# Turning h with transposing DMAs and moving the sum q_rot ahead of the maxima, in a cross-attention kernel on Trainium2

## The chip, the cores and the metric

The kernel runs on one core of a Trainium2 chip. The time is the device time of one execution in microseconds; the number quoted is the median of three runs. TensorE (PE), VectorE (DVE), ScalarE (ACT), GpSimd (POOL) and SyncE (SP) each run their own instruction stream and are tied together by semaphores alone. In this kernel SyncE does nothing but issue DMAs.

## The reference

Cross-attention with a residual, for 32 batches of 512 rows of x and 77 rows of context, width 512, 16 heads of 32:

```python
h = x * rsqrt(mean(x * x, -1) + EPS) * norm_w
q = rope(h @ Wq.T);  k, v = encoder_out @ Wkv.T;  k = rope(k)
attn = softmax(q . k / sqrt(32));  out = attn . v
return x + out @ Wo.T
```

x, the context, the weights and the result are float32. `rope(t)` is `t * cos + rotated(t) * sin`, where `rotated` swaps the two halves of each head of 32 and changes the sign of one.

## The kernel before

Every float32 operand of the large products is split into a float16 high part and a float16 low part (the value less its high part), and a product is taken as high x high + high x low + low x high. So each of the two 512x512 projections of 128 columns is twelve matmuls (L927 for q, L1002 for the output).

A setup block turns the weights and the context, makes all keys and values, and stores them in DRAM; between its steps it already treats the first rows of x (`fill` steps). Then comes the attention block. Its unit of work is one group of four heads of one batch (`unit`, 32 x 4 = 128 of them). A *slot* is one turn of the loop body; slot s = 4 i + g holds, on each engine, one step of many units at different stages. `t.unit(lag)` gives the unit that entered `lag` slots ago: lag 0 is the q projection, lag 1 the maxima, lag 4 the scores and exponentials, lag 5 the value product, lag 6 the turning of the output, lag 9 the output projection, lag 10 the residual; the negative lags -9 and -8 are the squares and the normalising of rows of x two batches ahead. Each engine executes its steps of a slot in the order in which they are written. `wait_ge(semaphore, count)` holds the engine until the semaphore has reached the count.

Orders within a slot, as written before the change:

- **TensorE:** scores (L912), q projection into the PSUM bank a_ps (L927), turning of o (L940), scores for the maxima (L954), value product (L972, L973, L975), turning of one quarter of h of the next batch into a_ps (`turn`, L161), output projection (L1002), turning of the maxima into a_ps (L1017).
- **VectorE:** q_rot = cos_part + sin_part of the *previous* slot's unit (L1112), residual (L1120), reciprocal (L1129), o_norm (L1133), low part of one head's probabilities (L1145), cos product (L1152) and the swap of halves (L1153), both out of a_ps, low part of o (L1158), reduction of the maxima (L1164), in the slots with g = 2 the low part of v (L1170), low part of h out of a_ps (`low`, L175).
- **ScalarE:** copy of the maxima (L1030), high part of q (L1036), exponentials (L1042), squares of x (L134), high part of o (L1051), high part of the probabilities (L1056), with g = 2 the high part of v (L1062), high part of h (`high`, L169), normalising (`normalise`, L154).
- **GpSimd:** low part of q (L1083), the two small steps of the root (L141, L145), sin product (L1091), low part of three heads' probabilities (L1095).
- **SyncE:** the maxima row into q_stack (L846), with odd g half a batch of results out (L852), with g = 1 x of three batches ahead (L857), v (L862) and k (L866), with g = 3 the residual's x (L871) and k_diag (L816), with even g twelve transfers that stack two groups of q (L830).

h's way in the old kernel: ScalarE writes x_norm (f32), TensorE turns it by four transposes per slot (f32) into a PSUM bank, ScalarE copies that to the f16 high part, VectorE subtracts for the low part. All four quarters of a batch are turned in the four slots of the batch before it. TensorE's L1017 writes into the same bank a_ps and therefore waits for h's low part (`h_lo`).

Of the kernel before, what the change touches and what calls it, by code (L numbers as in the profile page):

```python
# [6 lines left out]
F16 = mybir.dt.float16  # L7
ALU = mybir.AluOpType
# [4 lines left out]
P = 128  # L13
# [87 lines left out]
class Input:  # L101


    def __init__(self, nc, ctx, x, ident):
# [11 lines left out]
        self.x_norm = sb("x_norm", [P, 2, TT, D])  # L116
# [6 lines left out]
        self.turned = sem("turned")  # L123
        self.h_hi = sem("h_hi")
        self.h_lo = sem("h_lo")
# [11 lines left out]
    def root(self, pool, t):  # L137
# [6 lines left out]
        wait_from_first(pool, self.normed, t.s + 6)  # L144
# [12 lines left out]
    def turn(self, pe, t, bank):  # L157

        b, half, par = t.batch(1)
        for j in range(TT):  # L160
            mm = self.nc.tensor.transpose(bank[:, j * P:(j + 1) * P],  # L161
                                          self.x_norm[:, par, j, t.g * P:(t.g + 1) * P], self.ident)
        mm.then_inc(self.turned, 1)

    def high(self, act, t, bank):

        b, half, par = t.batch(1)
        act.wait_ge(self.turned, t.s + 5)
        self.nc.scalar.activation(self.h_t[:, par, 0, t.g, :], bank[:, :], ACT.Copy).then_inc(self.h_hi, 1)  # L169

    def low(self, dve, t, bank):

        b, half, par = t.batch(1)
        dve.wait_ge(self.h_hi, t.s + 5)
        self.nc.vector.tensor_tensor(self.h_t[:, par, 1, t.g, :], bank[:, :], self.h_t[:, par, 0, t.g, :],  # L175
                                     ALU.subtract).then_inc(self.h_lo, 1)


def setup_block(nc, sb_keep, stores, inp, x_ctx, norm_w, w_q, w_kv, w_o, consts_in, k_hi_dram, k_lo_dram, v_dram):
# [52 lines left out]
    with ExitStack() as ctx:  # L232
# [94 lines left out]
        def _(sp):  # L327
# [39 lines left out]
            for step in order:  # L367
# [10 lines left out]
                elif step[0] == "fill" and step[1].i == -1 and step[1].g == 0:  # L378
                    sp.wait_ge(inp.normed, TT)
                    sp.dma_start(inp.x_in[:, 0, :, :], inp.x_load[2]).then_inc(inp.x_got[0], 16)  # L380
# [4 lines left out]
        def _(pe):  # L385
            pe.wait_ge(ident_in, 16)
            pe.wait_ge(set_ready, 6)
            for step in order:
# [49 lines left out]
                elif step[0] == "fill" and step[1].batch_ok(1):  # L438
                    t = step[1]
                    if t.g == 0:  # L440
                        pe.wait_ge(inp.normed, TT)
                        pe.wait_ge(n_copied, CT)
                    wait_from_first(pe, inp.h_lo, t.s + 4)
                    inp.turn(pe, t, hp)
# [29 lines left out]
        def _(act):  # L474
# [21 lines left out]
            for step in order:  # L496
# [29 lines left out]
                elif step[0] == "fill":  # L526
# [3 lines left out]
                    if t.batch_ok(1):  # L530
                        inp.high(act, t, hp)
# [49 lines left out]
        def _(dve):  # L581
# [17 lines left out]
            for step in order:  # L599
# [94 lines left out]
                elif step[0] == "fill" and step[1].batch_ok(1):  # L694
                    inp.low(dve, step[1], hp)
# [5 lines left out]
def attention_block(nc, sb_keep, stores, inp, x, out, k_hi_dram, k_lo_dram, v_dram):  # L701
# [23 lines left out]
    with ExitStack() as ctx:  # L725
# [4 lines left out]
        h_t, h_lo = inp.h_t, inp.h_lo  # L730
# [26 lines left out]

        def turn_bank(t):

            return o_ps[:, 0, :] if not t.steady and t.s < SPARE else a_ps[:, :]  # L760
# [50 lines left out]
        def _(sp):  # L811
# [26 lines left out]
            def slot(t):  # L838
# [56 lines left out]
        def _(pe):  # L895
            def slot(t):
# [19 lines left out]
                if t.has(0):  # L916
                    if g == 0:
                        pe.wait_ge(h_lo, 4 * i + 4)
# [4 lines left out]
                    if not t.steady and s > SPARE:  # L923
                        wait_from_first(pe, h_lo, min(s + 4, UNITS))
# [53 lines left out]
                if t.batch_ok(1):  # L978
# [241 lines left out]
```

## Time and profile before

| | |
|---|---|
| median of three runs | 1513.55 us (1513.32 to 1514.33) |
| the profiled execution's own time | 1510.65 us |
| its span, first to last instruction | 1508.9 us |
| PE busy | 1342.6 us, 89% |
| DVE busy | 1285.7 us, 85% |
| ACT busy | 955.9 us, 63% |
| POOL busy | 869.0 us, 58% |
| L161, h's transposes, in the attention loop | 480 matmuls, 284 ns each |
| L169 / L175, h's high and low part | 120 each, 582 / 688 ns |
| L154, normalising | 128, 717 ns |
| L1095, POOL | 128, 3095 ns |
| L1112, DVE | 128, 2075 ns |
| L1164, DVE | 128, 1431 ns |

The difference between the profiled execution's own time and its span lies before the first and after the last instruction. Busy shares are means over the whole span. Matmuls are pipelined, so a group's mean is longer than the distance between its starts. The setup takes the first 213 us or so; the loop over 128 units follows, with a few slots of filling and emptying at its ends.

### The profile page before, as it was taken

What the parts mean: (1) busy time and instruction counts of PE and PEld (TensorE: products, weight loads), DVE (VectorE), ACT (ScalarE), POOL (GpSimd) and SP (SyncE); (2) the same over time, 40 slices, a digit from 0 to 9 for tenths busy, and PEclk for the clock granted to TensorE, in tenths of its full rate; (3) what the DMA queues carried; (4) which work ended last, traced back from release to release, by engine and by line L of the source; (5) the groups of instructions that cost most, each with busy time, mean ns of one, the idle gap of its engine ahead of it and who ended that gap; (6) DMA issues with size and microseconds to landing.
All of it is one profiled execution on the core that took longest, in us unless ns stands there. A gap on an engine that the chain in (4) does not pass through costs nothing.

```text
span 1508.9 us, 35021 instructions
## 1 busy us (share of the span) xinstructions
PE 1342.6 (89%) x12104; PEld 767.3 (51%) x12104; DVE 1285.7 (85%) x1696; ACT 955.9 (63%) x1330; POOL 869.0 (58%) x738
## 2 busy tenths in 40 slices
PE   2887777899999999999999999999999999999987
PEld 1443343455555555555555555555555555555544
DVE  3755567899999999999999999999999999999984
ACT  2623346677667776677766777676777667776652
POOL 1324456666666566665666656666666666665552
PEclk9998898999999999999999999999999999999999
DMA  3423244455545454555555554545555555453442
GB/s 129 150 94 103 93 100 97 105 131 138 135 137 136 119 131 117 133 136 131 136 133 138 138 138 124 132 117 133 136 131 136 131 136 137 118 131 92 112 124 84
DMA packets 171564, 187.53 MB, mean 124 GB/s; under 512 B 91152, under 2 KB 145552, under 8 KB 163312
## 3 DMA queue, kind: packets, MB, share of 16 engines
q1 hardware_dynamic: 168720, 181.70, 45.8%
q10 hardware_dynamic: 2784, 5.05, 0.9%
q8 instruction: 35, 0.57, 0.2%
q14 instruction: 25, 0.20, 0.1%
HBM read 92.16 MB, written 43.65 MB: 90 GB/s over the span
## 4 chain that ended last, share of the span: by engine, by line
ACT 28%; PE 25%; DVE 17%; issue 15%; ACTq 1%; DVEq 1%
DVE q_rot L1112 13%; PE a_ps L927 11%; ACT p_part L1056 10%; ACT probs L1042 10%; PE b_ps L1002 4%; PE score_ps L912 3%; ACT h_t L169 3%; ACT o_part L1051 3%; ACT junk L134 2%; DVE h_t L175 1%; PE b_ps L940 1%; ACT v_part L1062 1%; PE a_ps L1002 1%; PE score_ps L954 1%; ACTq L74 1%
## 5 line engine op out<-in xcount | busy, mean ns | idle before, releaser
L1095 POOL TENSOR_TENSOR p_part<-probs,p_part 77x1536 f16<-77x1536 f32 x128 | 396.1, 3095 | 35.2 <-ACT p_part L1056 25.3
L927 PE MATMUL a_ps<-h_t,wq 128*128 128x512 f16 x1536 | 384.8, 404 | 6.8 <-PEq L232 3.1
L1002 PE MATMUL b_ps<-wo,o_part 128*128 128x512 f16 x1464 | 338.3, 381 | 0.0
L1083 POOL TENSOR_TENSOR q_part<-q_rot,q_part 128x512 f16<-128x512 f32 x128 | 148.3, 1158 | 207.4 <-ACT q_part L1036 207.4
L1112 DVE TENSOR_TENSOR q_rot<-cos_part,sin_part 128x512 f32<-128x512 f32 x128 | 265.6, 2075 | 0.8 <-POOL sin_part L1091 0.8
L927 PEld LDWEIGHTS a_ps<-h_t,wq 128*128 128x128 f16 x1536 | 158.0, 103 | 211.9 <-issue 52.2
L1042 ACT ACTIVATE probs<-score_ps,scales 77x2048 f32<-77x2048 f32 x128 | 250.1, 1954 | 8.8 <-PE score_ps L912 7.6
L1056 ACT ACTIVATE p_part<-probs 77x2048 f16<-77x2048 f32 x128 | 243.6, 1903 | 0.0
L1002 PEld LDWEIGHTS b_ps<-wo,o_part 128*128 128x128 f16 x1464 | 143.5, 98 | 147.6 <-issue 3.2
L1091 POOL TENSOR_TENSOR sin_part<-swapped,consts 128x512 f32<-128x512 f32 x128 | 163.6, 1278 | 65.4 <-DVE swapped L1153 65.4
L1164 DVE TENSOR_REDUCE maxima<-score_ps 128x16 f16<-128x1232 f32 x128 | 183.2, 1431 | 1.9 <-PE score_ps L954 1.9
L972 PE MATMUL o_ps<-v_part,p_part 77*128 77x33 f16 x2048 | 168.9, 178 | 3.9 <-DVE p_part L1145 3.9
L1030 ACT ACTIVATE max_row<-a_ps 16x128 f16<-16x128 f16 x120 | 32.1, 268 | 217.6 <-PE a_ps L1017 217.6
L975 PE MATMUL o_ps<-v_part,p_part 77*128 77x33 f16 x2048 | 168.3, 177 | 0.0
L973 PE MATMUL o_ps<-v_part,p_part 77*128 77x32 f16 x2048 | 168.2, 177 | 0.0
L972 PEld LDWEIGHTS o_ps<-v_part,p_part 77*128 77x128 f16 x2048 | 160.5, 96 | 9.0 <-DVE p_part L1145 4.6
L973 PEld LDWEIGHTS o_ps<-v_part,p_part 77*128 77x128 f16 x2048 | 158.4, 96 | 4.2
L975 PEld LDWEIGHTS o_ps<-v_part,p_part 77*128 77x128 f16 x2048 | 157.8, 96 | 0.0
L1036 ACT ACTIVATE q_part<-q_rot 128x512 f16<-128x512 f32 x128 | 80.9, 632 | 115.0 <-DVE q_rot L1112 113.7
L1152 DVE TENSOR_TENSOR cos_part<-a_ps,consts 128x512 f32<-128x512 f32 x128 | 87.4, 683 | 66.2 <-PE a_ps L927 66.1
L912 PE MATMUL score_ps<-q_stack,k_stack 97*77 97x512 f16 x512 | 137.7, 392 | 0.1
L1145 DVE TENSOR_TENSOR p_part<-probs,p_part 77x512 f16<-77x512 f32 x128 | 132.0, 1031 | 0.0
(118 smaller groups left out, 2068.4 us busy)
## 6 DMA issues: line engine op xcount, KB each, us to landing
q_stack<-q_part SPq DMA_DIRECT2D x756, 64.0 KB, 2.1
x_in<-x SPq DMA_DIRECT2D x32, 1024.0 KB, 6.7
res<-x SPq DMA_DIRECT2D x32, 1024.0 KB, 5.9
out<-res SPq DMA_DIRECT2D x64, 512.0 KB, 3.5
v_sb<-v_dram SPq DMA_DIRECT2D x32, 154.0 KB
k_stack<-k_hi_dram SPq DMA_DIRECT2D x64, 77.0 KB, 7.1
c_nat<-ctx SPq DMA_DIRECT2D x19, 256.0 KB, 2.8
v_dram<-v_row ACTq DMA_DIRECT2D x19, 256.0 KB, 2.1
```

Of the source, the lines that this page charges most:

```text
L912: mm = nc.tensor.matmul(score_ps[0:S, j, :], k_stack[:, par, J * h + j, :], q_stack[:, h, j, :], start=True, stop=True)
L927: mm = nc.tensor.matmul(a_ps[:, :], wq[:, w, k, g * P:(g + 1) * P], h_t[:, t.parity, h, k, :], start=(k == 0 and w == 0 and h == 0), stop= ...
L972: nc.tensor.matmul(cell, hi, v_part[:, par, head, 0:HD + 1], start=True, stop=False)
L973: nc.tensor.matmul(cell[:, 0:HD], hi, v_part[:, par, head, HD + 1:2 * HD + 1], start=False, stop=False)
L975: mm = nc.tensor.matmul(cell, lo, v_part[:, par, head, 0:HD + 1], start=False, stop=True)
L1002: mm = nc.tensor.matmul(projection_bank(t, 0)[:, :], o_part[:, par, o, k, j * P:(j + 1) * P], wo[:, w, k, :], start=(k == 0 and o == 0 and ...
L1042: nc.scalar.activation(probs[:, g % 2, :, :], score_ps[0:S, :, :], ACT.Exp, scale=exp_scale[0:S, :]).then_inc(exped, 1)
L1056: nc.scalar.activation(p_part[:, g % 2, 0, :, :], probs[:, g % 2, :, :], ACT.Copy).then_inc(p_hi, 1)
L1091: nc.gpsimd.tensor_tensor(sin_part[:, :], swapped[:, :], sin_q, ALU.mult).then_inc(q_sin, 1)
L1095: nc.gpsimd.tensor_tensor(p_part[:, g % 2, 1, LO_V:J, :], probs[:, g % 2, LO_V:J, :], p_part[:, g % 2, 0, LO_V:J, :], ALU.subtract).then_i ...
L1112: nc.vector.tensor_tensor(q_rot[:, :], cos_part[:, :], sin_part[:, :], ALU.add).then_inc(q_full, 1)
L1164: nc.vector.tensor_reduce(maxima[:, :, :].rearrange("p j q -> p q j"), score_ps[:, :, 0:J * S].rearrange("p q (j k) -> p q j k", k=S), AX. ...
```

## The change

h is no longer turned on TensorE. ScalarE's normalising now writes the f16 high part directly, in x's own layout (`h_nat`, part 0). VectorE makes the low part from x and that high part, also in x's layout (lag -7, one slot after the normalising), directly ahead of the cos product. SyncE then turns both parts with two transposing DMAs per slot (lag -4, three slots after the low part) into `h_t`, placed behind the load of x and ahead of the loads of v and k. TensorE's q projection waits for the DMAs' semaphore at the first unit of a batch. The semaphores `turned`, `h_hi` and `h_lo` go; L1017 waits for the swap (`q_read`) instead of h's low part.

The second edit is VectorE's sum q_rot: it leaves the head of the next slot and stands in its own slot, between the low part of o and the reduction of the maxima.

```diff
-        self.x_norm = sb("x_norm", [P, 2, TT, D])
+        self.h_nat = sb("h_nat", [P, 2, 2, TT, D], F16)
@@ root
-        wait_from_first(pool, self.normed, t.s + 6)
+        wait_from_first(pool, self.h_low, t.s + 6)
@@ normalise
         if j == 0:
-            wait_from_first(act, self.turned, 4 * (b - 2) + 4)
-        self.nc.scalar.activation(self.x_norm[:, par, j, :], self.x_in[:, par, j, :], ACT.Copy,
+            wait_from_first(act, self.h_got[par], 16 * 2 * TT * half)
+        self.nc.scalar.activation(self.h_nat[:, par, 0, j, :], self.x_in[:, par, j, :], ACT.Copy,
                                   scale=self.rstd[:, j:j + 1]).then_inc(self.normed, 1)
+    def low(self, dve, t):
+        b, half, par, j = t.unit(-7)
+        dve.wait_ge(self.normed, t.s + 8)
+        self.nc.vector.scalar_tensor_tensor(out=self.h_nat[:, par, 1, j, :], in0=self.x_in[:, par, j, :],
+                                            scalar=self.rstd[:, j:j + 1], in1=self.h_nat[:, par, 0, j, :],
+                                            op0=ALU.mult, op1=ALU.subtract).then_inc(self.h_low, 1)
+    def turn(self, sp, t):
+        b, half, par, j = t.unit(-4)
+        for part in range(2):
+            sp.dma_start_transpose(self.h_t[:, par, part, :, j * P:(j + 1) * P],
+                                   self.h_nat[:, par, part, j, :]).then_inc(self.h_got[par], 16)
@@ SyncE, slot
-                    wait_from_first(sp, inp.normed, 4 * (b - 2) + 4)
+                    wait_from_first(sp, inp.h_low, 4 * (b - 2) + 4)
                     settle(t)
                     sp.dma_start(inp.x_in[:, par, :, :], inp.x_load[b]).then_inc(inp.x_got[par], 16)
+                if t.has(-4):
+                    b, half, par, j = t.unit(-4)
+                    sp.wait_ge(inp.h_low, s + 5)
+                    settle(t)
+                    if j == 0:
+                        wait_from_first(sp, q_done, 4 * (b - 2) + 4)
+                        settle(t)
+                    inp.turn(sp, t)
@@ TensorE, slot
                     if g == 0:
-                        pe.wait_ge(h_lo, 4 * i + 4)
+                        pe.wait_ge(inp.h_got[par], 16 * 2 * TT * (half + 1))
-                if t.batch_ok(1):
-                    ...
-                    inp.turn(pe, t, turn_bank(t))
-                    elif t.batch_ok(1) and (t.steady or s >= SPARE):
-                        pe.wait_ge(h_lo, s + 5)
-                    elif t.has(0) and s >= SPARE:
+                    elif t.has(0) and (t.steady or s >= SPARE):
                         pe.wait_ge(q_read, s + 1)
@@ ScalarE, slot
-                if t.batch_ok(1):
-                    inp.high(act, t, turn_bank(t))
@@ VectorE, slot
-                if t.has(1):
-                    dve.wait_ge(q_sin, s)
-                    dve.wait_ge(q_read, s)
-                    wait_from_first(dve, q_lo, s - 1)
-                    nc.vector.tensor_tensor(q_rot[:, :], cos_part[:, :], sin_part[:, :], ALU.add).then_inc(q_full, 1)
+                if t.has(-7):
+                    inp.low(dve, t)
                 if t.has(0):
                     dve.wait_ge(q_done, s + 1)
                     ...
+                if t.has(0):
+                    dve.wait_ge(q_sin, s + 1)
+                    dve.wait_ge(q_read, s + 1)
+                    wait_from_first(dve, q_lo, s)
+                    nc.vector.tensor_tensor(q_rot[:, :], cos_part[:, :], sin_part[:, :], ALU.add).then_inc(q_full, 1)
                 if t.has(1):
                     dve.wait_ge(max_mm, s)
-                if t.batch_ok(1):
-                    inp.low(dve, t, turn_bank(t))
```

The `fill` steps of the setup are changed in the same way.

## Rows read from the trace of the kernel before

**Rows 1.** The page, first line: span and instructions.

```profile
span 1508.9 us, 35021 instructions
```

**Rows 2.** Timeline, DVE, two slots: start us, us, engine, line, op [idle before].

```profile
803.17 1.43 DVE L1164 TENSOR_REDUCE maxima<-score_ps 128x16 f16<-128x1232 f32 x1
...
805.45 2.60 DVE L1112 TENSOR_TENSOR q_rot<-cos_part,sin_part 128x512 f32<-128x512 f32 x1
...
809.52 0.98 DVE L1145 TENSOR_TENSOR p_part<-probs,p_part 77x512 f16<-77x512 f32 x1
...
812.30 1.43 DVE L1164 TENSOR_REDUCE maxima<-score_ps 128x16 f16<-128x1232 f32 x1
...
814.13 3.06 DVE L1170 SCALAR_TENSOR_TENSOR v_part<-v_sb,scales,v_part 77x512 f16<-77x512 f32 x1 [0.39 <-ACT v_part L1062]
...
817.71 0.67 DVE L1112 TENSOR_TENSOR q_rot<-cos_part,sin_part 128x512 f32<-128x512 f32 x1
...
823.37 0.69 DVE L1152 TENSOR_TENSOR cos_part<-a_ps,consts 128x512 f32<-128x512 f32 x1 [2.54 <-PE a_ps L927]
...
825.20 1.44 DVE L1164 TENSOR_REDUCE maxima<-score_ps 128x16 f16<-128x1232 f32 x1
```

**Rows 3.** Timeline, DVE L1164: first two, first and last of the even stretch.

```profile
218.13 1.42 DVE L1164 TENSOR_REDUCE maxima<-score_ps 128x16 f16<-128x1232 f32 x1
...
223.80 1.43 DVE L1164 TENSOR_REDUCE maxima<-score_ps 128x16 f16<-128x1232 f32 x1
...
297.45 1.42 DVE L1164 TENSOR_REDUCE maxima<-score_ps 128x16 f16<-128x1232 f32 x1
...
1365.73 1.43 DVE L1164 TENSOR_REDUCE maxima<-score_ps 128x16 f16<-128x1232 f32 x1
```

**Rows 4.** Timeline, POOL, the same slots.

```profile
804.41 3.09 POOL L1095 TENSOR_TENSOR p_part<-probs,p_part 77x1536 f16<-77x1536 f32 x1
...
824.80 1.29 POOL L1091 TENSOR_TENSOR sin_part<-swapped,consts 128x512 f32<-128x512 f32 x1 [2.16 <-DVE swapped L1153]
...
826.27 3.09 POOL L1095 TENSOR_TENSOR p_part<-probs,p_part 77x1536 f16<-77x1536 f32 x1 [0.18 <-ACT p_part L1056]
```

**Rows 5.** Timeline, PE, from the long slot on.

```profile
817.84 0.22 PE L1017 MATMUL a_ps<-ident,maxima 128*16 128x128 f16 x1 [2.16 <-DVE h_t L175]
...
818.89 4.44 PE L927 MATMUL a_ps<-h_t,wq 128*128 128x512 f16 x12
...
825.33 0.64 PE L161 MATMUL a_ps<-consts,x_norm 128*128 128x128 f32 x4
...
825.80 2.75 PE L1002 MATMUL b_ps<-wo,o_part 128*128 128x512 f16 x12
...
829.53 2.75 PE L927 MATMUL a_ps<-h_t,wq 128*128 128x512 f16 x12
```

**Rows 6.** Windows: stretch, us, busy of PE, PEld, DVE, ACT, POOL, PEclk, DMA share, GB/s.

```profile
819.50:823.00 3.50, 3.50 (x11) 1.23 (x9) 1.32 (x2) 2.17 (x3) 1.52 (x3) 0.54 0.72 252
...
812.30:852.60 40.30, 37.99 (x363) 21.68 (x360) 36.67 (x46) 27.81 (x38) 25.00 (x21) 0.96 0.50 129
...
852.60:891.20 38.60, 36.34 (x365) 21.37 (x362) 36.66 (x47) 27.88 (x38) 25.05 (x21) 1.00 0.53 135
```

**Rows 7.** Timeline, DVE and POOL, two places of the setup.

```profile
173.38 0.70 DVE L593 SCALAR_TENSOR_TENSOR k_part<-k_rot,k_gain,k_part 128x462 f16<-128x462 f32 x1
...
173.49 1.60 POOL L573 TENSOR_TENSOR k_sin_part<-k_swapped,n_sin 128x462 f32<-128x462 f32 x1 [0.92 <-issue]
...
203.83 0.71 DVE L593 SCALAR_TENSOR_TENSOR k_part<-k_rot,k_gain,k_part 128x154 f16<-128x154 f32 x1 [0.54 <-ACT k_part L488]
...
203.85 0.51 POOL L323 TENSOR_TENSOR k_rot<-k_cos_part,k_sin_part 128x154 f32<-128x154 f32 x1
```

**Rows 8.** Timeline, SP's DMA issues, one pair of slots.

```profile
850.41 7.72 SPq L830 DMA_DIRECT2D q_stack<-q_part  x12
...
861.25 1.85 SPq L816 DMA_DIRECT2D k_diag<-k_hi_dram  x4
```

More of the change, by code:

```diff
@@ L122, in __init__ @@
         self.normed = sem("normed")
-        self.turned = sem("turned")
-        self.h_hi = sem("h_hi")
-        self.h_lo = sem("h_lo")
+        self.h_low = sem("h_low")
+        self.h_got = [sem(f"h_got{n}") for n in range(2)]
     def square(self, act, t):
@@ L152, in normalise @@
         if j == 0:
-            wait_from_first(act, self.turned, 4 * (b - 2) + 4)
-        self.nc.scalar.activation(self.x_norm[:, par, j, :], self.x_in[:, par, j, :], ACT.Copy,
+            wait_from_first(act, self.h_got[par], 16 * 2 * TT * half)
+        self.nc.scalar.activation(self.h_nat[:, par, 0, j, :], self.x_in[:, par, j, :], ACT.Copy,
                                   scale=self.rstd[:, j:j + 1]).then_inc(self.normed, 1)
[L157 to L176, printed above, removed]
+    def low(self, dve, t):
[9 more added lines that the diff above has]
+                                   self.h_nat[:, par, part, j, :]).then_inc(self.h_got[par], 16)
 def setup_block(nc, sb_keep, stores, inp, x_ctx, norm_w, w_q, w_kv, w_o, consts_in, k_hi_dram, k_lo_dram, v_dram):
@@ L377, in _ @@
                         load_w(O)
-                elif step[0] == "fill" and step[1].i == -1 and step[1].g == 0:
-                    sp.wait_ge(inp.normed, TT)
-                    sp.dma_start(inp.x_in[:, 0, :, :], inp.x_load[2]).then_inc(inp.x_got[0], 16)
+                elif step[0] == "fill" and step[1].has(-4):
+                    sp.wait_ge(inp.h_low, step[1].s + 5)
+                    inp.turn(sp, step[1])
+                    if step[1].g == 1:
+                        sp.wait_ge(inp.h_low, TT)
+                        sp.dma_start(inp.x_in[:, 0, :, :], inp.x_load[2]).then_inc(inp.x_got[0], 16)
             store_keys(NK - 2)
@@ L437, in _ @@
                     mm.then_inc(k_done, 1)
[L438 to L444, printed above, removed]
         def item(step):
@@ L529, in _ @@
                         inp.square(act, t)
-                    if t.batch_ok(1):
-                        inp.high(act, t, hp)
                     if t.has(-8):
@@ L693, in _ @@
                         key_low(n - 1)
-                elif step[0] == "fill" and step[1].batch_ok(1):
-                    inp.low(dve, step[1], hp)
+                elif step[0] == "fill" and step[1].has(-7):
+                    inp.low(dve, step[1])
             if NK % 3 == 0:
@@ L728, in attention_block @@
         sem = lambda name: ctx.enter_context(nc.semaphore(name))
-        h_t, h_lo = inp.h_t, inp.h_lo
+        h_t = inp.h_t
         swapped = sb("swapped", [P, T])
@@ L756, in attention_block @@
         PROJECT = 9
-        def turn_bank(t):
-            return o_ps[:, 0, :] if not t.steady and t.s < SPARE else a_ps[:, :]
         def projection_bank(t, lag):
@@ L917, in slot @@
                     if g == 0:
-                        pe.wait_ge(h_lo, 4 * i + 4)
+                        b, half, par = t.batch(0)
+                        pe.wait_ge(inp.h_got[par], 16 * 2 * TT * (half + 1))
                     if t.steady or s > PROJECT:
@@ L922, in slot @@
                         wait_from_first(pe, q_read, s)
-                    if not t.steady and s > SPARE:
-                        wait_from_first(pe, h_lo, min(s + 4, UNITS))
                     for k in range(KT):
@@ L976, in slot @@
                     mm.then_inc(valued, 1)
-                if t.batch_ok(1):
-                    b, half, par = t.batch(1)
-                    if g == 0:
-                        pe.wait_ge(inp.normed, 4 * b + 4)
-                    if t.has(0) and (t.steady or s >= SPARE):
-                        pe.wait_ge(q_read, s + 1)
-                    if not t.steady:
-                        wait_from_first(pe, h_lo, s + 4)
-                    inp.turn(pe, t, turn_bank(t))
                 if t.has(9):
@@ L1172, in slot @@
                         scalar=v_gain[0:S, :], in1=v_part[:, par, :, 0:HD], op0=ALU.mult, op1=ALU.subtract).then_inc(v_lo, 1)
-                if t.batch_ok(1):
-                    inp.low(dve, t, turn_bank(t))
             run(dve, slot)
```

## The prediction

> **What bounds the kernel now.** I first took the span [rows 1] and the busy shares of the page. TensorE and VectorE both stand near nine tenths, so the shares settle nothing, and I went on to the timelines of one batch of four slots. Read a slot from the start of one maxima reduction (L1164) to the next. A common slot is 9.13 us (803.17 to 812.30), the one behind the v low part 12.90 (812.30 to 825.20) [rows 2]. In the even stretch the first and the last reduction shown, 297.45 and 1365.73, are 27 batches apart [rows 3]: 39.57 us for a batch.
>
> In a common slot the reader is to see VectorE held by GpSimd. L1112, the sum q_rot, starts at 805.45 and takes 2.60 us; GpSimd's L1095 ran from 804.41 to 807.50, and q_rot ends 0.55 behind it [rows 2, 4]. The one at 817.71, with nothing in its way, takes 0.67 [rows 2]; I take 0.68 for a free one. In the long slot L1095 holds L1170, the v low part (3.06 us from 814.13). Behind it on VectorE stands h's low part, for which TensorE's transpose L1017 waits, 2.16 us idle; after that L927 takes 4.44 us instead of 2.75 [rows 2, 5]. The windows tell why: from 819.50 the granted clock is 0.54 of full, near its lower level of 1.2 GHz. A batch with this fall takes 40.30 us, one without 38.60 [rows 6]. A mean of 39.57 puts the fall, at 1.70 us, in 57% of the batches: 0.97 per batch.
>
> **The change part by part.** (1) TensorE loses four f32 transposes per slot (L161). L1002 starts 0.47 us behind their first [rows 5]; that is what they are worth of a TensorE that never idles in a common slot. ScalarE loses the copy of the high part (L169), for which only h's low part waited.
>
> (2) VectorE's low part stays one instruction, but with two SBUF inputs instead of PSUM and SBUF. That makes it of L1170's kind, held for 3.06 us behind L1095 [rows 2]. Free of that, the nearest rows are L1112's 0.67 and L593's 0.70 [rows 2, 7]; I take 0.74, with the bounds 0.67 and 3.06. It stands behind L1145 and ahead of the cos product.
>
> (3) q_rot moves ahead of the reduction of its slot and now waits for GpSimd's sin product of the same slot. Let T be the end of L927. In the long slot, where T is 823.33, the sin product runs from T+1.47 to T+2.76, and L1095, released by ScalarE's L1056, starts at T+2.94 [rows 4, 5]. With some 0.03 for the release (an estimate from the 0.04 between T and the cos product at 823.37 [rows 2]) q_rot starts at T+2.79, 0.15 us ahead of L1095. Who gets in first decides. L593 started 0.11 ahead of a GpSimd instruction and kept its 0.70, while GpSimd's stretched to 1.60; another that started 0.02 ahead ended 0.18 behind GpSimd's, so it had lost [rows 7]. 0.15 should do. Then q_rot takes 0.68, L1095 waits for it and ends near T+6.42; the reduction starts at T+3.39 and ends at T+4.82; L1017 follows 0.05 later, L927 1.05 after L1017, 2.75 long [rows 5]. The next T is 8.66 after the last. TensorE's own work, 9.13 less 0.47, is as long. VectorE keeps up: res, reciprocal and o_norm take 1.47, from 808.05 to L1145's start at 809.52 [rows 2], L1145 is held to T+6.97, the low part, if L1083 comes between, to T+8.5. A common slot: 8.66 instead of 9.13.
>
> The Trainium skill (SBUF — State Buffer, Who interferes with whom) says that whichever of the two engines issues first gets the shared pair for the whole instruction. The case of 0.02 goes against the letter of that; by the rule any lead would do, by these rows one of 0.11.
>
> (4) The long slot stays and changes its cause. The v low part now stands directly behind the reduction, still held by L1095. From the start of that reduction, L1095 ends at 3.03 and L1170 at 3.58. Then 1.47 for res to o_norm, 0.60 for L1145 and 0.66 for the low part, from start to start, bring the cos product to 6.31, where T is at 5.27: VectorE is 1.04 late. So the sin product ends at T+3.8; L1095, ready at T+2.94, follows it at once and beats q_rot, which is held for 3.09 + 0.55. The next reduction starts at 12.50. TensorE has then idled 3.0 us instead of 2.16. The slot: 12.50, against 11.20 (12.90 less 1.70) without the clock's fall.
>
> A batch without a fall is 3 x 8.66 + 12.50 = 38.48, against 38.60: what three common slots gain the long one gives back. For the fall the bounds are none and every batch (0 to 1.70); longer idling makes it no rarer, so I take 1.15, near the 0.97 of now. 39.63 against 39.57: +0.06 x 31 = +2 us.
>
> (5) SyncE issues eight transposing DMAs per batch, two in each slot, ahead of the k, v, res and q_stack transfers. No row shows one. From the start of twelve q_stack issues at 850.41 to the end of the k_diag issues at 863.10 are 12.7 us; two such halves, and two single issues more, are 26.8 of 39.6 us [rows 8]. The nearest row is q_stack's 0.64 per issue: eight make 5.2, hidden in the 12.8 that are free; from 1.4 each they are not. I take the q_stack row, so 0, and keep the other side as a rival. A transpose has most of a slot to land in before its q projection.
>
> (6) At the start the first two reductions are 5.67 apart [rows 3]; q_rot now stands in that chain, 8.66 less the 0.9 of the absent score matmuls, 7.8. Two such slots, +4. The setup loses sixteen transposes on TensorE, -1.
>
> The sum is +2 + 4 - 1 = +5 on the profiled execution's 1510.65 us (span 1508.9 [rows 1] and 1.75 around it). The median of the runs, 1513.55, is 2.9 above it: **1518 us**.
>
> **The rivals.** (A) SyncE or the DMA engines become the bound: slower. Place: SyncE's queue ahead of the q_stack issues. Price: a batch of 28 + 8c, with c per issue, deciding from c = 1.4; c = 2 gives 44 and +4.4 x 31, 1650; c = 3 some 1900. For it: an instruction that no row shows, and a queue two thirds full. Against: the issues seen take 0.46 and 0.64 [rows 8]. The transfers too could be slow: the DMA engines are half busy [rows 6], which leaves 19 us per batch, 2.4 per transpose.
>
> On this the Trainium skill (VectorE: DVE Perf Modes, The three transpose paths) gives 1309 ns for the DMA path at 128x128 against 390 ns on TensorE. Estimate from that page: 32 blocks per batch, 42 us if they add up; with the 20 of now, 62 per batch and 2200 us in all. No run here shows it yet.
>
> (B) q_rot loses its lead in every slot: slower. L1095 from T+2.94 to T+6.03, q_rot to T+6.58, the reduction from T+6.50: a slot of 11.8, a batch of 47, +7.5 x 31, about 1750. For it: the lead is thin, and the low part, held by L1083, can be late. Against: both ends of the race hang on the same L927, so the lead hardly scatters.
>
> (C) The long slot goes too, because q_rot wins also behind the v low part: faster. Then it is 8.66 + 1.04 = 9.7 and the clock never falls; batch 35.7, -3.9 x 31, about 1397. For it: VectorE need only be 0.9 less late. Against: in my sum L1095 is ready 0.8 us before the sin product ends.
>
> **How the numbers follow.** Forecast 0.53, with its own range 1485 to 1540: a fall in every batch is +17, none -34. A 0.27, B 0.08, C 0.12. This measurement can tell 0.2%, 3 us, from no change. Within the forecast's 0.53 I give faster 0.13, same 0.16, slower 0.24. Faster 0.13 + 0.12 = 0.25; same 0.16; slower 0.24 + 0.27 + 0.08 = 0.59. The range leaves out C and the far end of A: 1485 to 1750.
>
> **What would show it.** Right: L1112 at 0.68 in three slots of four and above 3.5 in the one behind L1170; reductions 8.7, 8.7, 8.7 and 12.5 apart; L1095 behind q_rot and stretched by 0.4; L1017 waiting some 3 us for the reduction in the long slot. Step 5 is wrong if TensorE waits for a DMA ahead of L912 or L927, or if SyncE has no idle time; step 3 if L1112 is long everywhere; step 4 if no slot is over 10 us, or if the fall of the clock costs much more than 1.15 per batch.

## The result, and the profile after

The changed kernel takes 1620.46 us, the median of four runs (1620.18 to 1621.34), beside 1513.43 for the kernel before (1511.60 to 1514.33, four runs). The ratio is 1.071, with a 95% interval of 1.069 to 1.073: slower, by 107 us. The forecast was 1518, in a range of 1485 to 1750.

From the page of the profile after, the span, the granted clock by slices (in tenths) and SyncE's DMA queue (packets, MB, share of the 16 engines):

```profile
span 1618.4 us, 34120 instructions
...
PEclk9998877899999999999999999999999999999999
...
q1 hardware_dynamic: 307984, 215.29, 58.7%
```

In the kernel before the same queue had 168,720 packets and 45.8% of the DMA engines' span.

The reductions that answer to [rows 3] are L1143 now (start us, us, engine, line, operation):

```profile
224.64 1.43 DVE L1143 TENSOR_REDUCE maxima<-score_ps 128x16 f16<-128x1232 f32 x1
...
321.72 1.44 DVE L1143 TENSOR_REDUCE maxima<-score_ps 128x16 f16<-128x1232 f32 x1
...
1469.58 1.44 DVE L1143 TENSOR_REDUCE maxima<-score_ps 128x16 f16<-128x1232 f32 x1
```

The last two are 108 slots apart, as are 297.45 and 1365.73 before: 42.51 us for a batch instead of 39.57, and 27 batches lose 79.6 us. The first reduction is 6.5 us late; from it to the second row are 97.1 us instead of 79.3; the rest after the third row adds 5.7. That is the 109.5 by which the span grew: three quarters of it in the even stretch, a sixth in the filling.

The lines of the changed kernel: on TensorE L903 is the scores, L917 the q projection, L930 the turning of o, L982 the output projection and L995 the turning of the maxima (L1017 before); on GpSimd L1059 is the low part of q, L1067 the sin product and L1071 the low part of three heads' probabilities (L1095 before). They move by a few lines in the runs below.

A long slot of VectorE and the one behind it, which answer to [rows 2] (idle before, and its releaser, in brackets):

```profile
616.48 0.69 DVE L1138 TENSOR_TENSOR q_rot<-cos_part,sin_part 128x512 f32<-128x512 f32 x1 [0.83 <-POOL sin_part L1067]
617.09 1.44 DVE L1143 TENSOR_REDUCE maxima<-score_ps 128x16 f16<-128x1232 f32 x1
618.44 3.35 DVE L1149 SCALAR_TENSOR_TENSOR v_part<-v_sb,scales,v_part 77x512 f16<-77x512 f32 x1
...
624.52 0.68 DVE L1125 TENSOR_TENSOR cos_part<-a_ps,consts 128x512 f32<-128x512 f32 x1
...
627.24 3.57 DVE L1138 TENSOR_TENSOR q_rot<-cos_part,sin_part 128x512 f32<-128x512 f32 x1 [0.81 <-POOL sin_part L1067]
630.73 1.43 DVE L1143 TENSOR_REDUCE maxima<-score_ps 128x16 f16<-128x1232 f32 x1
...
643.00 1.44 DVE L1143 TENSOR_REDUCE maxima<-score_ps 128x16 f16<-128x1232 f32 x1
...
651.75 1.44 DVE L1143 TENSOR_REDUCE maxima<-score_ps 128x16 f16<-128x1232 f32 x1
```

q_rot (L1138) takes 0.69 at 616.48; the common slot is 8.75 us (643.00 to 651.75). The v low part (L1149) is held 3.35 us, and q_rot at 627.24 for 3.57. The long slot is 13.64, and the slot behind it 12.27 here. GpSimd in the same place, which answers to [rows 4]:

```profile
616.64 3.49 POOL L1071 TENSOR_TENSOR p_part<-probs,p_part 77x1536 f16<-77x1536 f32 x1 [0.20 <-ACT p_part L1034]
620.09 1.16 POOL L1059 TENSOR_TENSOR q_part<-q_rot,q_part 128x512 f16<-128x512 f32 x1
...
627.17 3.09 POOL L1071 TENSOR_TENSOR p_part<-probs,p_part 77x1536 f16<-77x1536 f32 x1
```

L1071 starts 0.16 us behind q_rot and is stretched by 0.4; in the long slot it starts at 627.17, ahead of q_rot. TensorE, which answers to [rows 5]:

```profile
619.69 2.75 PE L917 MATMUL a_ps<-h_t,wq 128*128 128x512 f16 x12
623.47 0.65 PE L930 MATMUL b_ps<-consts,o_norm 128*128 128x128 f32 x4 [1.02 <-DVE o_norm L1103]
...
626.48 2.76 PE L982 MATMUL b_ps<-wo,o_part 128*128 128x512 f16 x12 [0.65 <-DVE o_part L1131]
632.29 0.27 PE L995 MATMUL a_ps<-ident,maxima 128*16 128x128 f16 x1 [3.04 <-DVE maxima L1143]
633.21 1.92 PE L903 MATMUL score_ps<-q_stack,k_stack 97*77 97x512 f16 x4 [0.64 <-issue]
634.92 4.69 PE L917 MATMUL a_ps<-h_t,wq 128*128 128x512 f16 x12
```

From the long slot on TensorE idles three times, 1.02, 0.65 and 3.04 us: 4.7 against the 2.16 before. The last of the three, for the reduction, ends in the slot behind. Then L917 takes 4.69. The windows of the same slots, which answer to [rows 6] (stretch, us, busy of PE, PEld, DVE, ACT, POOL, granted clock, DMA share, GB/s):

```profile
617.09:630.73 13.64, 10.31 (x92) 5.27 (x90) 12.79 (x13) 7.06 (x10) 9.21 (x6) 1.00 0.62 181
630.73:643.00 12.27, 10.07 (x80) 5.21 (x81) 7.67 (x13) 6.18 (x8) 3.52 (x5) 0.72 0.32 71
643.00:651.75 8.75, 8.58 (x86) 4.90 (x85) 7.87 (x12) 6.47 (x9) 6.61 (x6) 1.00 0.62 194
632.00:638.00 6.00, 5.07 (x13) 1.93 (x14) 3.87 (x6) 3.36 (x5) 1.21 (x2) 0.50 0.22 44
```

From 632 to 638 the granted clock is 0.50, the lower level of 1.2 GHz. The slot behind the long one is mostly 10.7 or 12.3 us in turn, with a granted clock of 0.84 or 0.72: none of the 27 batches is without slow matmuls. SyncE, which answers to [rows 8]:

```profile
623.56 2.59 SPq L168 DMA_TRANSPOSE h_t<-h_nat  x2
...
634.06 2.54 SPq L168 DMA_TRANSPOSE h_t<-h_nat  x2
```

Two transposing DMAs (L168) take 2.54 to 2.59 us to issue, 1.27 each.

### The profile page after: what moved, and what is told of

Read it like the earlier page. It is cut to its first block and busy times, and to the rows that moved or that the text cites. A ratio compares the mean times of both kernels' runs of the same rounds, so it can differ in the third digit from the quotient of the medians.

```text
span 1618.4 us, 34120 instructions
## 1 busy us (share of the span) xinstructions
PE 1340.6 (83%) x11592; PEld 726.7 (45%) x11592; DVE 1269.6 (78%) x1696; ACT 898.7 (56%) x1202; POOL 902.6 (56%) x738
## 5 line engine op out<-in xcount | busy, mean ns | idle before, releaser
L1071 POOL TENSOR_TENSOR p_part<-probs,p_part 77x1536 f16<-77x1536 f32 x128 | 429.4, 3355 | 36.9 <-ACT p_part L1034 36.8
L917 PE MATMUL a_ps<-h_t,wq 128*128 128x512 f16 x1536 | 409.1, 423 | 4.3 <-PEq L225 2.9
L982 PE MATMUL b_ps<-wo,o_part 128*128 128x512 f16 x1464 | 337.2, 380 | 18.5 <-DVE o_part L1131 18.4
L917 PEld LDWEIGHTS a_ps<-h_t,wq 128*128 128x128 f16 x1536 | 166.3, 108 | 235.1 <-issue 93.4
L1067 POOL TENSOR_TENSOR sin_part<-swapped,consts 128x512 f32<-128x512 f32 x128 | 163.0, 1274 | 192.5 <-DVE swapped L1126 192.5
L1138 DVE TENSOR_TENSOR q_rot<-cos_part,sin_part 128x512 f32<-128x512 f32 x128 | 180.6, 1411 | 108.8 <-POOL sin_part L1067 108.8
L1059 POOL TENSOR_TENSOR q_part<-q_rot,q_part 128x512 f16<-128x512 f32 x128 | 148.2, 1158 | 114.3 <-ACT q_part L1014 114.3
L982 PEld LDWEIGHTS b_ps<-wo,o_part 128*128 128x128 f16 x1464 | 133.9, 98 | 167.3 <-DVE o_part L1131 21.6
L1143 DVE TENSOR_REDUCE maxima<-score_ps 128x16 f16<-128x1232 f32 x128 | 183.6, 1434 | 0.1
L1115 DVE TENSOR_TENSOR p_part<-probs,p_part 77x512 f16<-77x512 f32 x128 | 177.1, 1384 | 0.0
L903 PE MATMUL score_ps<-q_stack,k_stack 97*77 97x512 f16 x512 | 158.6, 439 | 9.7 <-issue 9.7
L1029 ACT ACTIVATE o_part<-b_ps 128x512 f16<-128x512 f32 x128 | 76.4, 597 | 148.7 <-PE b_ps L930 148.7
```

The costliest lines, as they stand in the source:

```text
L917: mm = nc.tensor.matmul(a_ps[:, :], wq[:, w, k, g * P:(g + 1) * P], h_t[:, t.parity, h, k, :], start=(k == 0 and w == 0 and h == 0), stop= ...
L982: mm = nc.tensor.matmul(projection_bank(t, 0)[:, :], o_part[:, par, o, k, j * P:(j + 1) * P], wo[:, w, k, :], start=(k == 0 and o == 0 and ...
L1067: nc.gpsimd.tensor_tensor(sin_part[:, :], swapped[:, :], sin_q, ALU.mult).then_inc(q_sin, 1)
L1071: nc.gpsimd.tensor_tensor(p_part[:, g % 2, 1, LO_V:J, :], probs[:, g % 2, LO_V:J, :], p_part[:, g % 2, 0, LO_V:J, :], ALU.subtract).then_i ...
L1115: nc.vector.tensor_tensor(p_part[:, u, 1, 0:LO_V, :], probs[:, u, 0:LO_V, :], p_part[:, u, 0, 0:LO_V, :], ALU.subtract).then_inc(p_lo_v, 1)
L1138: nc.vector.tensor_tensor(q_rot[:, :], cos_part[:, :], sin_part[:, :], ALU.add).then_inc(q_full, 1)
```

## The experiments

Times are medians beside the kernel before on the same chip (1511.8 to 1513.0 us there). "A batch" is the mean over the same 27 batches as above, read off the reductions of each trace.

**One edit at a time.** q_rot_back keeps the DMAs and undoes the second edit:

```diff
@@ VectorE, head of the slot
+                if t.has(1):
+                    dve.wait_ge(q_sin, s)
+                    ...
+                    nc.vector.tensor_tensor(q_rot[:, :], cos_part[:, :], sin_part[:, :], ALU.add).then_inc(q_full, 1)
@@ VectorE, ahead of the reduction
-                if t.has(0):
-                    dve.wait_ge(q_sin, s + 1)
-                    ...
-                    nc.vector.tensor_tensor(q_rot[:, :], cos_part[:, :], sin_part[:, :], ALU.add).then_inc(q_full, 1)
```

> The changed kernel with q_rot back at the head of the next slot: the transposing DMAs and VectorE's moved low part stay. Theory 1 (the loss comes from the long slot: the v low part makes VectorE late, q_rot loses to GpSimd's L1071 and the clock falls in every batch): without q_rot ahead of the reduction that chain is cut, and h's low part, no longer behind the v low part, holds no TensorE transpose up. Common slots 8.7 to 9.2 us, the long one near 11, a batch 37 to 39, the kernel 1440 to 1510 us. Theory 2 (the transposing DMAs cost it, by SyncE's queue or the q_stack rows that land late): the kernel stays within 30 us of the changed one, 1590 to 1650.

q_rot_only is the kernel before with the reverse of this diff.

> The kernel of before with one edit alone: q_rot ahead of the reduction in its own slot; h is still turned on TensorE. Theory 1: the loss is there without any transposing DMA. Common slots 9.1 to 9.2 us with q_rot at 0.7, a long slot of 13 to 14 with q_rot held 3.6 us, and a slow stretch of TensorE behind each: a batch 41.5 to 43.5, the kernel 1580 to 1640 us. Theory 2: no slower than before by more than what the long slot gained, 1490 to 1540.

| | h turned on TensorE | h turned by DMAs |
|---|---|---|
| q_rot at the head of the next slot | 1513.0 (before) | 1490.5, ratio 0.986 (0.983 to 0.989) |
| q_rot ahead of the reduction | 1577.8, ratio 1.043 (1.039 to 1.046) | 1620.5 (after), ratio 1.071 |

The DMAs alone are a gain of 22 us, q_rot's move alone a loss of 65; together they cost 107, which is 65 more than the two added up. Theory 2, that the DMAs themselves are the loss, falls. (In spans q_rot_only is 70.4 us longer than before: 38.6 in the even stretch and 31.8 outside it.)

In q_rot_back the slots are 9.3 to 9.7 us in the mean and the long one 9.9, not 8.7 to 9.2 and 11: VectorE works nearly without a pause, and TensorE keeps its full clock. The window of 160 us (VectorE is the third engine):

```profile
620.00:780.00 160.00, 147.98 (x1390) 80.52 (x1389) 157.13 (x187) 106.71 (x138) 104.16 (x83) 1.00 0.75 162
```

and VectorE in a common slot, where q_rot is held 3.1 us; in the long slot the v low part is, and q_rot takes 0.68:

```profile
725.72 1.42 DVE L1143 TENSOR_REDUCE maxima<-score_ps 128x16 f16<-128x1232 f32 x1
727.07 3.11 DVE L1088 TENSOR_TENSOR q_rot<-cos_part,sin_part 128x512 f32<-128x512 f32 x1
```

In q_rot_only I had the sign and nearly the size (a batch of 41.00, 1577.8 us; the ranges began at 41.5 and 1580), but not the mechanism. q_rot is never held there, 0.69 in the long slot as well. h's low part still stands behind the v low part on VectorE, and TensorE waits for it, as it did before the edit. VectorE's long slot there, with the line numbers of the kernel before:

```profile
734.44 2.23 DVE L1170 SCALAR_TENSOR_TENSOR v_part<-v_sb,scales,v_part 77x512 f16<-77x512 f32 x1
736.60 0.68 DVE L175 TENSOR_TENSOR h_t<-a_ps,h_t 128x512 f16<-128x512 f32 x1
...
743.92 0.69 DVE L1159 TENSOR_TENSOR q_rot<-cos_part,sin_part 128x512 f32<-128x512 f32 x1 [0.83 <-POOL sin_part L1091]
```

and TensorE in the same slot:

```profile
737.33 0.22 PE L1017 MATMUL a_ps<-ident,maxima 128*16 128x128 f16 x1 [2.40 <-DVE h_t L175]
```

The slot takes 11.4 us, or 13.1 where slow matmuls follow. That is nearly what it took before (11.2 or 12.9, after a wait of 2.16), so this wait isn't what the edit costs. The 1.43 us more per batch are 0.66 in the slot behind the long one, 0.24 in the other two, and 0.52 in the long slot, where the wait is 0.24 longer and the slow matmuls come in 20 of the 27 batches instead of 16. Why the slot behind it grows was not tested.

TensorE's wait of 2.40 us ahead of L1017 does something else: it makes the q projection and all that follows from it late, L1095 too, while VectorE catches up. So I read the two traces like this: that wait protected q_rot; the DMAs take it away, TensorE runs ahead of VectorE, and q_rot is lost. No run puts the wait alone back. What is shown is that q_rot is held in no slot of q_rot_only, and in the long slot of every batch of the changed kernel.

**What holds the v low part.** q_low_waits is the changed kernel with one wait:

```diff
@@ GpSimd, ahead of the low part of q (L1059)
+                    if g == 3 and t.batch_ok(0):
+                        pool.wait_ge(v_lo, t.i + 1)
```

> The changed kernel with one wait more: in the slot behind v, GpSimd's low part of q (L1059) waits for the v low part (L1149). Theory 1 (a waiting VectorE instruction loses the shared pair to GpSimd's next one when that follows within some 0.03 us): L1149 ends 0.6 us behind L1071 instead of 1.7, the long slot falls from 13.65 to 12.5 us, q_rot is still held 3.6 us in it and the slow matmuls behind it stay: a batch 41.3 to 41.7 instead of 42.6, the kernel 1580 to 1595 us. Rival: L1149 is simply that long, or the held low part of q makes q_stack late: the long slot stays at 13.6 or longer, 1615 us or more.

1573.4 us, ratio 1.042 (1.038 to 1.046), a batch of 40.88: the long slot as expected, the batch and the time below their ranges, since I had the slow matmuls stay as they were. VectorE's long slot:

```profile
730.57 1.44 DVE L1145 TENSOR_REDUCE maxima<-score_ps 128x16 f16<-128x1232 f32 x1
731.92 2.24 DVE L1151 SCALAR_TENSOR_TENSOR v_part<-v_sb,scales,v_part 77x512 f16<-77x512 f32 x1
...
739.61 3.57 DVE L1140 TENSOR_TENSOR q_rot<-cos_part,sin_part 128x512 f32<-128x512 f32 x1 [0.81 <-POOL sin_part L1069]
743.10 1.43 DVE L1145 TENSOR_REDUCE maxima<-score_ps 128x16 f16<-128x1232 f32 x1
```

and GpSimd's row beside it:

```profile
730.21 3.40 POOL L1073 TENSOR_TENSOR p_part<-probs,p_part 77x1536 f16<-77x1536 f32 x1 [0.28 <-ACT p_part L1034]
```

The v low part now ends 0.55 us behind GpSimd's L1073 (733.61), as it did in [rows 2]. The long slot is 12.53; q_rot is held as in the changed kernel, and the slow matmuls are fewer: the slot behind is mostly 10.7 or 11.1 instead of 10.7 or 12.3. In three early batches it keeps its full clock and takes 9.0 to 9.2, though TensorE has idled as long (3.2 to 3.4 us in that slot, as in the others). One of the three, in the order of the windows above:

```profile
581.04:590.06 9.02, 7.24 (x80) 4.47 (x81) 7.61 (x12) 6.27 (x8) 3.61 (x5) 1.00 0.38 98
```

So the length of the idling alone doesn't decide whether the clock falls.

The long slot shows who gets in at the hand-over between the two engines: of the waiting VectorE instruction and GpSimd's next one, which starts 0.04 us before its predecessor's end (620.09 against 620.13), GpSimd's went first in the changed kernel, and that was worth 1.1 us in the long slot.

**Who goes first, by a wait.** both_wait adds a second wait to that kernel:

```diff
@@ GpSimd, ahead of the low part of three heads (L1071)
                 if t.has(4):
+                    if t.has(0):
+                        pool.wait_ge(q_full, s + 1)
                     pool.wait_ge(p_hi, s - 3)
```

> The changed kernel with two waits more on GpSimd: the three-head low part (L1071) waits for q_rot of its slot, and in the slot behind v the low part of q waits for the v low part. Theory 1: q_rot takes 0.7 us in all four slots, the v low part ends some 0.6 us behind L1071 instead of 1.7, and the long slot is 9.7 to 11 us; a batch 36 to 38, bounded below by SyncE's 38.2 us of issues if these can't overlap: the kernel 1400 to 1490 us. Theory 2 (transposing DMAs): 1590 or more, since nothing of the DMAs changes. A third: L1071, started later, makes the low part of p late for TensorE's value matmuls, and the common slots grow from 8.75 to over 9.2.

1490.8 us, ratio 0.986 (0.983 to 0.989), a batch of 38.58, both just above their ranges. q_rot takes 0.69 in every slot, the slots are 8.93 and 9.95. But the slot behind the long one varies from 9.1 to 12.6 in the middle of the stretch, and here SyncE's issues are the reason. First its timeline, then TensorE's:

```profile
700.29 0.59 SPq L829 DMA_DIRECT2D q_stack<-max_row  x1
701.07 2.53 SPq L168 DMA_TRANSPOSE h_t<-h_nat  x2
703.86 7.73 SPq L813 DMA_DIRECT2D q_stack<-q_part  x12
...
738.44 0.58 SPq L829 DMA_DIRECT2D q_stack<-max_row  x1
```

```profile
717.09 2.76 PE L917 MATMUL a_ps<-h_t,wq 128*128 128x512 f16 x12 [1.79 <-DMA h_t<-h_nat]
```

SyncE goes from issue to issue, with no wait between them; the stretch from 700.29 to the same issue a batch later (738.44) is 38.2 us, all but the kernel's batch. TensorE waits 1.79 us for h_t.

no_v_low is the changed kernel without the v low part in the loop (ScalarE's high part of v then raises the semaphore of the low part in its place, and the two waits for it are put right; these lines are left out here):

```diff
-                if g == 2 and t.batch_ok(0):
+                if g == 2 and t.batch_ok(0) and not t.steady:
```

> The changed kernel without the low part of v on VectorE in the steady loop (its product with v's low part uses old values there). It prices the long slot: theory 1: all slots 8.7 to 8.8 us, no slow matmuls, TensorE never idle for over 0.3 us: a batch of 35.0 if TensorE sets it (1380 to 1400 us), or 38.2 and more if SyncE's issues then set it (1470 to 1500 us). Theory 2: a batch stays at 42 and more, over 1590 us.

1517.4 us, ratio 1.003 (1.002 to 1.005); a batch of 38.70 and common slots of 8.75. In the loop it is SyncE's bound again, as the second figure had it: SyncE has no pause between its issues, and TensorE waits for h_t. I had expected no slow matmuls and no idling; the slot behind the old long one takes 9.4 to 14.7 us, at a granted clock down to 0.77:

```profile
726.36 4.20 PE L917 MATMUL a_ps<-h_t,wq 128*128 128x512 f16 x12 [2.63 <-DMA h_t<-h_nat]
```

Outside the loop, where the v low part stays, the filling and the emptying keep what they had lost against the kernel before, 27.4 us (26.2 in q_rot_only). I had left these out.

two_waits_pe_turn puts q_rot's move and the wait of L1095 for it into the kernel before, without any transposing DMA.

> The kernel of before (h turned on TensorE, no transposing DMA) with q_rot ahead of the reduction and L1095 waiting for q_rot of its slot. Theory 1 (SyncE at 38.3 us per batch bounds both of the last fast kernels): here it has 27 us only, so TensorE sets common slots of 9.2 us, and the long one is 10.3 to 11.3: a batch 37.9 to 38.9, and with few slow matmuls 1460 to 1500 us. Rival: h's low part behind the held v low part still makes TensorE wait 2 us and the clock fall: a batch of 39.5 and more, over 1505 us.

1593.2 us, ratio 1.054 (1.050 to 1.058), a batch of 41.88: the rival was right. The v low part takes 2.52, L1017 waits for h's low part behind it and starts 2.4 us later behind the reduction than in a common slot, and in most batches the clock falls. TensorE's row:

```profile
699.23 0.22 PE L1017 MATMUL a_ps<-ident,maxima 128*16 128x128 f16 x1 [2.69 <-DVE h_t L175]
```

Of the two kernels in which the order was forced, it paid in the one where h is turned by DMAs.

**What the transposing DMAs cost.** waits_plain turns nothing and moves the same bytes, in both_wait:

```diff
-            sp.dma_start_transpose(self.h_t[:, par, part, :, j * P:(j + 1) * P],
-                                   self.h_nat[:, par, part, j, :]).then_inc(self.h_got[par], 16)
+            sp.dma_start(self.h_t[:, par, part, :, j * P:(j + 1) * P],
+                         self.h_nat[:, par, part, j, :].rearrange("p (k c) -> p k c", c=P)).then_inc(self.h_got[par], 16)
```

> The kernel with both GpSimd waits, its transposing DMAs replaced by plain ones of the same bytes (h isn't turned, so q is wrong). Theory 1 (SyncE is the bound of the kernel with both waits: 26.8 + 8 x 1.27 = 37.0 to 38.3 us): at 0.6 us per issue it has 5 us more, and a batch falls from 38.5 to the 36.4 to 36.7 of three slots of 8.9 and one of 9.9, the kernel to 1420 to 1440 us. Rival: the pair of VectorE and GpSimd, or TensorE, sets the 38.5: no change, 1485 to 1495 us. The DMA share tells how much of the transfer time is the turning: 0.75 with it.

waits_one_issue, also both_wait, lays h_nat out with both parts of a row side by side and turns them in one DMA:

```diff
-        for part in range(2):
-            sp.dma_start_transpose(...)
+        sp.dma_start_transpose(self.h_t[:, par, :, :, j * P:(j + 1) * P].rearrange("p w k c -> p (w k) c"),
+                               self.h_nat[:, par, j, :, :].rearrange("p w d -> p (w d)")).then_inc(self.h_got[par], 16)
```

> The kernel with both GpSimd waits, and the two transposing DMAs of a slot (128 x 512 each) made one of 128 x 1024. If the 1.27 us on SyncE are for an issue: SyncE has 5 us more per batch and the kernel takes 1420 to 1440 us. If they are for the blocks that it describes: one issue takes some 2.4 us and nothing changes, 1480 to 1495 us.

1449.3 us (ratio 0.959, 0.956 to 0.962) and 1446.7 us (0.958, 0.955 to 0.962): the same, and batches of 37.00 and 36.99. The forecast of 1420 to 1440 was too low by 9 and 7; the slot behind the long one stays at 9.0 or 9.5. The issues and a window of 160 us, of the plain kernel first, then of the one with one issue:

```profile
746.82 1.38 SPq L168 DMA_DIRECT2D h_t<-h_nat  x2
```

```profile
620.00:780.00 160.00, 151.23 (x1458) 84.65 (x1456) 143.26 (x194) 110.88 (x142) 112.48 (x87) 1.00 0.71 167
```

```profile
743.65 1.29 SPq L167 DMA_TRANSPOSE h_t<-h_nat  x1
```

```profile
620.00:780.00 160.00, 151.61 (x1460) 85.05 (x1459) 143.37 (x195) 113.16 (x143) 112.73 (x87) 1.00 0.73 163
```

An issue of 128 x 1024 costs 1.29 us here; over the even stretch the medians of the four slots are 1.35, 1.27, 1.36 and 1.84. One of 128 x 512 costs 1.26 in the median, a plain one 0.64: the price is mostly per issue. Not all of the 5 us came free: the transposing issues take 6.0 instead of 10.3 us of a batch, but those of k's low part (L857 in both_wait, L856 here) 1.8 instead of 0.85, and all issues together 29.4 instead of 32.4. And the DMA share is 0.71 without and 0.73 with turning, so here the turning asks the DMA engines for little more than the copying does.

one_issue does the same to the changed kernel, without the waits:

> The changed kernel with one transposing DMA of 128 x 1024 per slot in place of two, and no wait added on GpSimd. SyncE then has some 33 us of work in a batch of 42.6. Theory 1 (in the changed kernel SyncE isn't on the path; VectorE's held v low part and q_rot are): only TensorE's waits for q_stack go, 0.2 to 0.5 us per batch, and the kernel takes 1600 to 1620 us. Rival (SyncE's queue has a large part in the loss, also by making the clock fall longer): 1590 us or less.

1618.8 us, ratio 1.070 (1.068 to 1.072), a batch of 42.51, to the hundredth the changed kernel's. SyncE has no part in the loss. That also fells a reading in this expectation: the 0.64 us that TensorE idles ahead of L903 at 633.21 are no late q_stack, since they stay (0.79 in the same place here).

q_rot_back_one does it to q_rot_back:

> q_rot back at the head of the next slot, and one transposing DMA per slot. In the kernel with q_rot back VectorE works without a pause (9.33 us common, 9.94 long): theory: it bounds that kernel, not SyncE, so nothing changes, a batch of 38.0 to 38.4 and 1478 to 1492 us. Rival (SyncE bounds it as it does the kernel with both waits): a batch of 37 or less and 1450 us or less.

1472.8 us, ratio 0.975 (0.973 to 0.976); a batch of 38.02 instead of 38.53. The batch is in its range and the time 5 us below: neither "nothing changes" nor the rival. The common and the long slots keep their 9.33 and 9.93, with VectorE as their bound. The two spans are 20.6 us apart. 13.5 of that lie in the even stretch, more than half of it in two single slots of q_rot_back, of 14.3 and 12.3 us; 7 lie ahead of the first reduction, and one trace of each doesn't tell whether they are the edit's.

**The two waits apart, and a last step.** p_wait_one_issue is waits_one_issue without the wait of q's low part.

> The kernel with both GpSimd waits and one transposing DMA per slot, less the wait of the low part of q for the v low part. Theory 1: L1149 is held through two GpSimd instructions again and ends 1.1 us later; q_rot still wins, so the long slot is 11.0 us instead of 9.95, the next keeps 9.0 to 9.5 or holds a few slow matmuls: a batch 38.1 to 38.8, the kernel 1478 to 1505 us. Rival (the order q_rot, then L1071 is all that counts): within 10 us of 1447.

1481.2 us, ratio 0.980 (0.978 to 0.982); a long slot of 11.07, a batch of 38.19. The hand-over again costs 1.1 us in the long slot, here with hardly a slow matmul behind it.

two_heads sets `LO_V = 2` in waits_one_issue.

> The kernel with both GpSimd waits and one transposing DMA per slot, with two heads of p's low part on VectorE and two on GpSimd instead of one and three. GpSimd's instruction shrinks from 3.1 to about 2.1 us, the v low part behind it ends a microsecond earlier, and VectorE's grows by 0.5 to 0.6: the long slot 9.3 to 9.6, the common ones 8.7 to 8.9, a batch 35.5 to 36.4 and 1400 to 1430 us. Rival (VectorE is as full as the pair): common slots over 9.0 us and 1450 us or more.

1433.3 us, ratio 0.9485 (0.947 to 0.950): the fastest of all, 79 us under the kernel before. The slots are 8.85 and 9.51, as expected; the batch of 36.50 and the time are just above their ranges (36.4 and 1430). VectorE's long slot:

```profile
715.02 0.69 DVE L1141 TENSOR_TENSOR q_rot<-cos_part,sin_part 128x512 f32<-128x512 f32 x1 [0.82 <-POOL sin_part L1068]
715.63 1.44 DVE L1146 TENSOR_REDUCE maxima<-score_ps 128x16 f16<-128x1232 f32 x1
716.98 1.56 DVE L1152 SCALAR_TENSOR_TENSOR v_part<-v_sb,scales,v_part 77x512 f16<-77x512 f32 x1
...
725.15 1.44 DVE L1146 TENSOR_REDUCE maxima<-score_ps 128x16 f16<-128x1232 f32 x1
```

and GpSimd's instruction in it, now of two heads:

```profile
715.87 2.12 POOL L1074 TENSOR_TENSOR p_part<-probs,p_part 77x1024 f16<-77x1024 f32 x1 [0.89 <-DVE q_rot L1141]
```

It takes 2.12 us instead of 3.09, and the v low part 1.56, with its end again 0.55 behind.

## Why the prediction was right in sign and short in size

The likeliest case put the loss of the loop in VectorE's long slot and the clock's fall behind it, and there it is; rivals A, B and C did not happen. The size was not right: 1518 against 1620. And part of the success is luck. The likeliest case had its own range of 1485 to 1540, which 1620 is far above; the stated range reached it only for the sake of A and B, which play no part here. The sign hung on a sum of +5 us, in a case that gave 0.24 of its 0.53 to slower; the rest of the 0.59 was A's and B's.

- **Steps 1 and 3, the common slot: right.** 8.75 for 8.66. q_rot starts 0.16 ahead of L1071 (0.15 predicted), takes 0.69, and L1071 is stretched by 0.4. Two such slots per batch: +0.2 us.
- **Step 2: right.** h's low part (L160) takes 0.74 in the common slots and in the long one.
- **Step 4, the long slot: the mechanism right, two terms too small.** q_rot lost to L1071 there, as forecast. But the v low part was to end 0.55 us behind L1071; it ends 1.66 behind, since L1059 goes first. That makes VectorE 2.08 us late (the q projection ends at 622.44, 619.69 + 2.75; the cos product starts at 624.52) instead of 1.04, and the slot 13.64 instead of 12.50. With the hand-over put right by a wait it is 12.53, near the number of the prediction (whose terms, added up again, give 12.6): +1.15 us per batch. The clock's fall is the other term. I took 1.15, near the old mean, by "longer idling makes it no rarer"; the slot behind the long one averages 11.36 us instead of 9.81 (42.51, less 2 x 8.75 and 13.65): +1.55. At full clock that slot takes 9.0 (q_low_waits), not 8.66, so 0.3 of the 1.55 is not the clock's, and the fall costs some 2.4 per batch instead of 1.15. The sum also had one stretch of idling, 3.0 us; that one came (3.04), and the waits for o_norm and o_part, 1.02 and 0.65, were missing in it. Before, the fall came in 16 of the 27 batches, after 2.16 us of idling; now in each, after 4.7. Where TensorE doesn't idle so (q_rot_back, waits_one_issue), the even stretch has a clock of 1.00. What decides between 10.7 and 12.3 stays open, as does the full clock in three batches of q_low_waits: that the longer idling brings the fall is the likely reading, not a shown one.
- The common slots, the hand-over and the slot behind the long one make 0.2 + 1.15 + 1.55 = 2.9 us per batch, the 42.51 less 39.63, and 27 x 2.9 = 78 of the 102 us missing.
- **Step 5, SyncE: right.** 1.27 us per issue, under the threshold of 1.4 and twice my 0.64; one_issue shows it costs nothing there. 28 + 8 x 1.27 = 38.2 became the bound only once the long slot was mended. (The 28 stands in the prediction without its working, beside a 26.8 from rows; the measured 38.2 bears out the 28.) The estimate of 2200 us, worked out from the 1309 ns per block that the Trainium skill gives (VectorE: DVE Perf Modes, The three transpose paths), fell with it: by that figure 32 blocks take 42 us if they add up, and waits_one_issue turns them in a batch of 36.99, beside all its other transfers. The times of single transposes don't add up.
- **Step 6, start and end: too small.** +17.8 us from the first reduction to the tenth where +4 was predicted. q_rot's move alone has 21.1 there, the DMAs alone 7.4. The first two slots of the filling were 5.7 us before, and the next seven 8.3 to 12.3; with q_rot ahead of the reduction the first two are 9.2 to 9.5 and the next seven 8.7 to 14.1, in both kernels that move q_rot, alone or with the DMAs. The granted clock is lower there too, 0.76 against 0.85 below, but it is 0.80 in q_rot_back, which loses far less. The end, too, is q_rot's: 5.1 of the 5.7 us are in q_rot_only. For the filling, the same 35 us before and after:

```profile
225.00:260.00 35.00, 27.12 (x201) 14.26 (x201) 25.41 (x32) 22.85 (x33) 21.58 (x20) 0.85 0.44 95
```

```profile
225.00:260.00 35.00, 18.03 (x59) 7.16 (x60) 17.97 (x22) 11.19 (x20) 12.56 (x14) 0.76 0.43 76
```

The 6.5 us ahead of the first reduction, for which I had -1, stay open. The first reduction now waits for a second q_rot, and q_rot_only has 5.7 of them with the setup untouched; but the two kernels with q_rot back differ in the same stretch by 7.0 (+4.4 and -2.7).

One slip stands in the range: a fall in no batch is 1.15 x 31 = 36 us less, not 34.

## What to carry to other kernels

When two edits each take away a wait, reckon the pair: a wait that costs 2 us may be what lets a slower engine catch up, and here both together lost 65 us more than the two apart. Where GpSimd and VectorE hold each other up and the order matters, set it by a semaphore rather than by a lead of 0.15 us; two waits turned a loss of 107 us into a gain of 22, and with half the transposing issues one of 65. Without the DMAs the same order, forced, was a loss of 81, so measure it in the kernel at hand. And when a stretch of idling grows, don't carry over its mean price for the clock: ask whether the fall now comes every time, and how long it lasts.

## What the hardware did that I had not expected

- At the end of a GpSimd instruction that has held VectorE, GpSimd's own next instruction gets in if it is ready: L1149, waiting since 618.44, stood back for L1059 at 620.09 and ended at 621.79. The Trainium skill (SBUF — State Buffer, Who interferes with whom) says that whoever issues first gets the shared pair, a sentence that it has of VectorE's two-port modes. VectorE's was 1.65 us older here, so either issuing isn't what I took it for or the rule doesn't cover a waiting one. I had read its one exception, 0.02 us in [rows 7], as a matter of leads alone.
- A transposing DMA from SBUF to SBUF costs 1.26 us of SyncE's time at 128 x 512 (median, both_wait) and 1.35 at 128 x 1024, f16 (waits_one_issue, with 1.84 in one slot of four); a plain one of 128 x 512 in 256-byte pieces 0.64 (waits_plain).
- TensorE's lower clock is not small change: the slot from 630.73 to 643.00 has a granted clock of 0.72 and takes 12.27 us, the same slot at full clock in q_low_waits 9.02.
